# Cross-attention scores from stacked high and low float32r parts, through a scratch in HBM

## What is computed

```
q = axial_rope((layernorm(x) @ Wq), pos)       # per batch 128 x 32 x 8
k, v = split(ctx @ Wkv);  k = axial_rope(k, pos)
w = softmax(einsum('bqhd,bkhd->bhqk', q, k) / sqrt(8))
x = x + einsum('bhqk,bkhd->bqhd', w, v) @ Wout + bout
```

## Time and profile before

| | |
|---|---|
| median of 3 runs | 776.66 us |
| profiled execution | 777.8 us |
| its span, first to last instruction | 776.0 us |
| mean granted TensorE clock | 0.921 of 2.4 GHz |
| self-attention, last score product (L479) | starts 162 us |
| cross-attention, shifted products (L787) | 189.6 to 383.5 us |
| mixture of experts | from 397 us |

### The profile page before, as it was taken

The page is one execution under the profiler, slowest core; times in us unless marked ns, Lnnn a source line. Parts: engine busy times, 40 slices in busy tenths (PEclk is TensorE's granted clock), DMA queues, the critical chain, the costliest instruction groups (busy, mean ns, idle before and its releaser), DMA issues. The chain is left out here.

```text
span 776.0 us, 18811 instructions
## 1 busy us (share of the span) xinstructions
PE 687.4 (89%) x6959; PEld 528.3 (68%) x6959; DVE 401.1 (52%) x917; ACT 301.4 (39%) x676; POOL 359.9 (46%) x451
## 2 busy tenths in 40 slices
PE   4799999876999999999757979299999999999975
PEld 4677777444887887877633868267777777777864
DVE  3546554326366666665257599542222222221998
ACT  1455655321244445444517423023333333333422
POOL 2357653332122212210027435547777777775634
PEclk9889999887599999999858989779999999999989
DMA  7000000012112111111046930113333333333931
GB/s 200 13 13 9 11 13 9 13 18 35 19 20 37 27 34 29 30 34 18 3 157 188 238 87 1 41 55 103 103 102 103 103 107 102 106 102 114 349 102 34
DMA packets 49558, 55.88 MB, mean 72 GB/s; under 512 B 8462, under 2 KB 43776, under 8 KB 49472
## 3 DMA queue, kind: packets, MB, share of 16 engines
q1 hardware_dynamic: 39124, 33.16, 16.1%
q0 software_dynamic: 7584, 20.72, 8.3%
q10 hardware_dynamic: 2764, 0.80, 0.5%
HBM read 34.34 MB, written 14.55 MB: 63 GB/s over the span
## 5 line engine op out<-in xcount | busy, mean ns | idle before, releaser
L1563 PE MATMUL s<-wx,routed_out 128*128 x316 | 109.1, 468 | 1.0 <-ACT routed_out L1266 1.0
L1434 DVE TENSOR_TENSOR routed_out<-s,routed_out 128x176 f32<-128x176 f32 x79 | 27.0, 342 | 141.9 <-ACT routed_out L1271 141.9
L1198 POOL DMA_INDIRECT slot_rows<-stage,dest x79 | 78.0, 987 | 35.5 <-issue 19.5
L735 ACT ACTIVATE b_pt<-s 128x1024 f32<-128x1024 f32 x64 | 63.5, 1020 | 79.0 <-PE s L787 79.0
L1164 POOL DMA_INDIRECT routed_in<-normed_rows,token x79 | 77.7, 983 | 31.0 <-issue 20.3
L1582 PE MATMUL last<-wx,routed_out 88*128 x316 | 81.5, 380 | 0.7 <-DVE routed_out L1439 0.7
L717 DVE TENSOR_REDUCE b_mx<-s 128x8 f32<-128x1024 f32 x32 | 39.2, 1225 | 75.9 <-PE s L832 75.9
L1563 PEld LDWEIGHTS s<-wx,routed_out 128*128 128x128 f32 x316 | 54.9, 194 | 18.8 <-issue 2.4
L1172 POOL TENSOR_TENSOR h_full<-h_full,silu_gate 128x512 f32<-128x512 f32 (+1 forms) x24 | 31.8, 1326 | 57.0 <-ACT h_full L1242 57.0
L1447 DVE SCALAR_TENSOR_TENSOR x_sb<-wx,share,x_sb 128x256 f32<-128x256 f32 x64 | 51.7, 825 | 11.9 <-DMA wx<-slot_rows 10.1
L1582 PEld LDWEIGHTS last<-wx,routed_out 88*128 88x128 f32 x316 | 53.7, 190 | 5.7 <-issue 1.5
(11 more groups left out here) (265 smaller groups left out, 1568.9 us busy)
## 6 DMA issues: line engine op xcount, KB each, us to landing
wx<-slot_rows SPq DMA_DIRECT2D x16, 512.0 KB, 8.8
b_qk<-b_rot SPq DMA_DIRECT2D x128, 32.0 KB
wx<-in_w_gate SPq DMA_DIRECT2D x4, 528.0 KB
wx<-in_w_up SPq DMA_DIRECT2D x4, 528.0 KB
wx<-in_w_down SPq DMA_DIRECT2D x4, 528.0 KB
x_sb<-in_x SPq DMA_DIRECT2D x4, 512.0 KB, 6.2
normed_rows<-stage SPq DMA_DIRECT2D x4, 512.0 KB, 3.9
out<-x_sb SPq DMA_DIRECT2D x16, 128.0 KB, 1.8
```

Source lines behind the costliest of these rows:

```text
L735: nc.scalar.activation(pt[:, c % 2, u].rearrange("p h q -> p (h q)"), s2[:, u].rearrange("p a n -> p (a n)"), ACT.Exp, scale=HD_B ** -0.5) ...
L1198: nc.gpsimd.indirect_dma_start(out=slot_rows[:, :], out_offset=bass.IndirectOffsetOnAxis(ap=dest[:, n:n + 1].bitcast(U32), axis=0), in_=ys ...
L1563: last = nc.tensor.matmul(s2[:, n % 2, 0, 0:2 * FE], xT[:, n % 2, P * k:P * k + P], wx[:, bass.ds(e, 1), 2 * FE * k:2 * FE * k + 2 * FE].r ...
```

## The change

q and k, after the rotation, are each split into a high part (rounded to float32r, ACT) and a low part (the rest, POOL), in `parts`: q high, q low, k high, k low. A strip of `qk` then holds 24 rows: (q high, k high), (q low, k high), (q high, k low), 8 rows each, and rows 24 and 25 take the high and low part of the negated maxima beside ones in k. So one float32r matmul per score product gives high.high + low.high + high.low; the product low.low is left out. The stacking goes through a scratch of two slots in HBM, `stacks`: six DMAs a batch (128 partitions x two runs of 128 floats each) write it, and one DMA of 1 MB reads a whole slot into `qk`. The slots are filled once from `qk` (ones) at the first step. The low part of the maxima is a DVE subtraction. The preparation begins two steps earlier (FIRST = -10), the moments, normed x and projection of a batch two steps ahead of before, the rotation too, the split and the six DMAs in c = 2b - 6, the gather in 2b - 5.

```
@@ self_attention
...
-        return (t - 1 - BEHIND + 7) // 2 + 1
+        return (t - 1 - BEHIND + g["cross"]["ahead"]) // 2 + 1
...
@@ cross_attention
-    qk = sb("b_qk", [P, SL, 8, 2, P])
+    stacks = nc.dram_tensor("b_stacks", [2, P, 16 * P], F32, kind="Internal").ap()
+    qk = sb("b_qk", [P, SL, 8, 2, P], F32R)
     rot = sb("b_rot", [P, 2, 2, 2, P])
+    parts = sb("b_parts", [P, 2, 2, 4, P], F32R)
...
-    mT = sb("b_mT", [NH_B, 2, P])
+    mT = sb("b_mT", [NH_B, 2, 2, P], F32R)
...
-    FIRST, LAST = -8, NH + 2
-    STACK = 16 * 8
-
-    g["cross"] = {"init": init, "zeroed": zeroed, "mx": mx, "qk": qk, "v": v, "xcT_done": xcT_done, "steps": (FIRST, LAST)}
+    FIRST, LAST = -10, NH + 2
+    ROWS, SHIFT = 3 * HD_B, 3 * HD_B + 2
+    PIECES = 16 * 6
+
+    g["cross"] = {"init": init, "mx": mx, "qk": qk, "v": v, "xcT_done": xcT_done, "ahead": 9, "steps": (FIRST, LAST)}
...
+    def stacked(b, seg, part):
+
+        rows = stacks[b % 2].rearrange("(i r f) (x w t) -> r i (f x) w t", i=4, r=8, x=8, w=2)[2 * seg + part]
+        first, step = ((0, 2), (1, 1), (0, 3))[seg]
+        return rows, parts[:, b % 2, part, first:first + step + 1:step, :].bitcast(F32)
+
     def sync(sp, c):
-        b = batch(c + 8)
+        if c == FIRST:
+            for i in range(2):
+                sp.dma_start(stacks[i].rearrange("p (x w t) -> p x w t", x=8, w=2), qk[:, i].bitcast(F32)).then_inc(stack_out[i], 16)
+        b = batch(c + 10)
         if b is not None:
             need(sp, trx_done, b - 1)
             sp.dma_start(ctx[:, b % 2, :], io["ctx"][b]).then_inc(ctx_in[b % 2], 16)
         b = turned(c)
         if b is not None:
-            sp.wait_ge(mT_out, b + 1)
-            sp.dma_start(qk[HD_B:P:32, b % SL, :, 0, :], mT[:, b % 2, :]).then_inc(mrow_in[b % 2], 16)
+            for part, done in ((0, mT_out), (1, mT_lo)):
+                sp.wait_ge(done, b + 1)
+                sp.dma_start(qk[ROWS + part:P:32, b % SL, :, 0, :].bitcast(F32), mT[:, b % 2, part, :].bitcast(F32)).then_inc(mrow_in[b % 2], 16)
+        b = batch(c + 6)
+        if b is not None:
+            if b < 2:
+                sp.wait_ge(stack_out[b], 16)
+            else:
+                sp.wait_ge(qk_in[(b - 2) % SL], 16 * ((b - 2) // SL + 1))
+            sp.wait_ge(rot_lo, b + 1)
+            for seg in range(3):
+                for part in range(2):
+                    rows, src = stacked(b, seg, part)
+                    sp.dma_start(rows, src).then_inc(stack_out[b % 2], 16)
         b = batch(c + 5)
         if b is not None:
             need(sp, s2_done, 2 * (b - SL) + 2)
-            for part in range(2):
-                sp.wait_ge(rot_done, 2 * b + part + 1)
-                for i in range(4):
-                    sp.dma_start(qk[32 * i + 4 * part:32 * i + 4 * part + 4, b % SL], rot[32 * i:32 * i + 32, b % 2, part]).then_inc(qk_in[b % SL], 16)
+            sp.wait_ge(stack_out[b % 2], 16 + PIECES * (b // 2 + 1))
+            sp.dma_start(qk[:, b % SL].bitcast(F32), stacks[b % 2].rearrange("p (x w t) -> p x w t", x=8, w=2)).then_inc(qk_in[b % SL], 16)
 
     def gpsimd(pool, c):
-        b = batch(c + 8)
+        b = batch(c + 10)
         if b is not None:
             pool.wait_ge(ln_aggr, b + 1)
             nc.gpsimd.tensor_tensor(rstd[:, b % 2, 0:1], mv[:, b % 2, 1:2], g["ln_eps"][:, 0:1], ALU.add).then_inc(eps_done, 1)
             pool.wait_ge(eps_done, b + 1)
             nc.gpsimd.tensor_tensor(rstd[:, b % 2, 1:2], rstd[:, b % 2, 0:1], g["ln_pow"][:, 0:1], ALU.pow).then_inc(rstd_done, 1)
-        b = batch(c + 5)
-        if b is not None:
-            pool.wait_ge(cos_done, b + 1)
+        b = batch(c + 7)
+        if b is not None:
             pool.wait_ge(sin_done, b + 1)
-            if b >= 2:
-                pool.wait_ge(qk_in[(b - 2) % SL], STACK * ((b - 2) // SL + 1))
+            need(pool, rot_lo, b - 1)
             nc.gpsimd.tensor_tensor(rot[:, b % 2, 0], by_cos[:, 0], by_sin[:, 1], ALU.subtract).then_inc(rot_done, 1)
             nc.gpsimd.tensor_tensor(rot[:, b % 2, 1], by_cos[:, 1], by_sin[:, 0], ALU.add).then_inc(rot_done, 1)
-        b = batch(c + 7)
+        b = batch(c + 6)
+        if b is not None:
+            pool.wait_ge(rot_hi, b + 1)
+            pool.wait_ge(rot_done, 2 * b + 2)
+            halves = parts[:, b % 2].rearrange("p a (w h) t -> p a w h t", h=2)
+            nc.gpsimd.tensor_tensor(halves[:, :, :, 1, :], rot[:, b % 2], halves[:, :, :, 0, :].bitcast(F32), ALU.subtract).then_inc(rot_lo, 1)
+        b = batch(c + 9)
         if b is not None:
             pool.wait_ge(xn_done, b + 1)
             nc.gpsimd.tensor_tensor(x[:, b, :], x[:, b, :], g["ob"][:, 1, :], ALU.add).then_inc(ob_added, 1)
...
-        b = batch(c + 5)
+        b = batch(c + 7)
         if b is not None:
             dve.wait_ge(proj_done, b + 1)
             need(dve, rot_done, 2 * b)
-            for table, dst, done in ((1, by_cos, cos_done), (0, by_sin, sin_done)):
-                nc.vector.tensor_tensor(dst[:].rearrange("p a w t -> p (a w) t"), mid[:].rearrange("p (a t) -> p a t", a=4),
-                                        g["rope"][:, table, b, :].unsqueeze(1).broadcast_to([P, 4, P]), ALU.mult).then_inc(done, 1)
-        b = batch(c + 7)
+            for table, dst in ((1, by_cos), (0, by_sin)):
+                last = nc.vector.tensor_tensor(dst[:].rearrange("p a w t -> p (a w) t"), mid[:].rearrange("p (a t) -> p a t", a=4),
+                                        g["rope"][:, table, b, :].unsqueeze(1).broadcast_to([P, 4, P]), ALU.mult)
+            last.then_inc(sin_done, 1)
+...
+        b = turned(c)
+        if b is not None:
+            dve.wait_ge(mT_out, b + 1)
+            if b >= 2:
+                dve.wait_ge(mrow_in[b % 2], 32 * (b // 2))
+            nc.vector.tensor_tensor(mT[:, b % 2, 1, :], s1[0:NH_B, 0, 0:P], mT[:, b % 2, 0, :].bitcast(F32), ALU.subtract).then_inc(mT_lo, 1)
...
@@ scalar
+        b = batch(c + 6)
+        if b is not None:
+            act.wait_ge(rot_done, 2 * b + 2)
+            if b >= 2:
+                act.wait_ge(stack_out[b % 2], 16 + PIECES * (b // 2))
+            nc.scalar.copy(parts[:, b % 2].rearrange("p a (w h) t -> p a w h t", h=2)[:, :, :, 0, :], rot[:, b % 2]).then_inc(rot_hi, 1)
         exps(c, 0)
         b = turned(c)
         if b is not None:
             act.wait_ge(mT_done, b + 1)
             if b >= 2:
-                act.wait_ge(mrow_in[b % 2], 16 * (b // 2))
-            nc.scalar.copy(mT[:, b % 2, :], s1[0:NH_B, 0, 0:P]).then_inc(mT_out, 1)
+                act.wait_ge(mrow_in[b % 2], 32 * (b // 2))
+            nc.scalar.copy(mT[:, b % 2, 0, :], s1[0:NH_B, 0, 0:P]).then_inc(mT_out, 1)
         exps(c, 1)
         b = batch(c - 2)
...
@@ tensor, shifted
-            pe.wait_ge(mrow_in[(h // 2) % 2], 16 * (h // 4 + 1))
+            pe.wait_ge(mrow_in[(h // 2) % 2], 32 * (h // 4 + 1))
             pe.wait_ge(max_done, 2 * min(h + 2, NH - 1) + 1)
             need(pe, exp_done, 2 * h)
             need(pe, v_out, min((h + 1) // 2, NB - 1) + 1)
-            need(pe, xcT_done, min((h + 6) // 2, NB - 1) + 1)
+            need(pe, xcT_done, min((h + 8) // 2, NB - 1) + 1)
             need(pe, oT_done, (h - 4) // 2 + 1)
             for n in range(4):
                 for i in range(4):
-                    rows = slice(32 * i, 32 * i + HD_B + 1)
+                    rows = slice(32 * i, 32 * i + SHIFT)
                     pair = qk[rows, (h // 2) % SL, 4 * (h % 2) + n]
                     last = nc.tensor.matmul(second_bank(i)[:, P * n:P * n + P], pair[:, 1, :], pair[:, 0, :], start=(n == 0), stop=(n == 3))
...
@@ tensor, scores
-                pe.wait_ge(qk_in[b % SL], STACK * (b // SL + 1))
+                pe.wait_ge(qk_in[b % SL], 16 * (b // SL + 1))
             if h == 0:
                 pe.wait_ge(before["exp_done"], 2 * NB)
                 pe.wait_ge(before["max_done"], 2 * NB)
                 pe.wait_ge(before["mT_out"], NB)
             need(pe, max_done, 2 * h)
-            need(pe, mT_out, h // 2)
+            need(pe, mT_lo, h // 2)
             if half(c):
                 pe.wait_ge(exp_done, 2 * c + 1)
             for n in range(4):
                 for i in range(4):
-                    pair = qk[32 * i:32 * i + HD_B, b % SL, 4 * u + n]
+                    pair = qk[32 * i:32 * i + ROWS, b % SL, 4 * u + n]
                     last = nc.tensor.matmul(first_bank(i)[:, P * n:P * n + P], pair[:, 0, :], pair[:, 1, :], start=(n == 0), stop=(n == 3))
             last.then_inc(s1_done, 1)
 
...
```

More of the change, by code:

```diff
@@ L619, in cross_attention @@
     ctx_in = [sem(f"ctx_in{i}") for i in range(2)]
-    (zeroed, init, ln_stats, ln_aggr, eps_done, rstd_done, xn_done, trx_done, xcT_done, proj_done, cos_done, sin_done, rot_done,
-     ob_added, vp_done, v_out, s1_done, max_done, mT_done, mT_out, s2_done, exp_done, pv_done, sums_out, tb_done, rc_done,
+    stack_out = [sem(f"b_stack_out{i}") for i in range(2)]
```

(22 more changed lines are left out.)

18 lines of the change are left out of this document (10 added, 8 removed).

## The result

The changed kernel takes 830.7 us (median of 4 runs, 826.07 to 839.84) against 776.76 us: ratio 1.0719, 95% interval 1.0662 to 1.0777. The forecast was 823, range 770 to 875. The profiled execution is the shortest of the four, 826.07 us; its span is 824.3 us, 48.3 us more than the span of before, while the medians are 53.9 us apart.

What follows compares the result with a forecast made beforehand. PE bounds the old kernel; four DMA engines would bound the changed cross stage. Fill +3.9, start +5, period +34.8, tail -3.6, clock +6 sum to +46: 777.8 + 46 - 1.1 = 823 us, range 770 to 875.

Steps and rivals of the forecast that it cites:

- The four engines: Writing pieces to the scratch: strip outermost keeps each on four DMA engines, 10.3 us for a batch's six pieces.
- The period: Cross-attention stage: DMA work served in order takes 15.5 us a batch against PE's 10.9; +34.8 us over 13 batches.
- I charge nothing: High-part copy on ACT and split on POOL, a step ahead of use: 0 us; without cover each costs its length.
- The clock: Cross stage: a wait of about 4.6 us each batch invites PE's drop to 1.2 GHz; 0 to 16 us, taken as 6.
- The start: Up to the first shifted product: +3.9 us for the fill, +5 for its rows standing behind the third batch's pieces.
- The preparation two steps earlier: About 2.2 us of PE work per batch moves from cross stage into PE-bound self-attention steps: nothing in sum.
- The groups: Score groups on PE: 1.11 us becomes 0.67 (bounds 0.45 and 1.11), saving 1.8 us a batch.
- The added wait for mT_lo: In every second half scores() waits on PE for the DVE subtraction: 0.35 to 0.6 us.
- The tail: Last three batches, without pieces, run at PE's pace: -3.6 us.
- rival 1: Pieces spread over 16 engines at 0.4 us each, so DMA hides behind PE: 759 us, chance 0.11.
- rival 2: Score groups stay at 1.11 us, pieces hidden, new waits remain, 12.4 us a batch: 786 us, chance 0.05.
- the forecast's own range: 800 us (pieces 9.3 us, no clock loss) to 875 (pieces at 53 GB/s, 14.8 us), chance 0.79.

Runs made afterwards that it cites:

- Experiments 1 and 2: 1: changed kernel, scratch reordered to 16 outermost, four gathers, no fill: 758.5 us, again 751.93. 2: the same without the reordering: 835.05 us.
- experiment 3: Changed kernel with three of the six pieces a batch: 762.11 us; with every piece written twice, 12 a batch: 965.9 us.
- experiment 7: Kernel before, with only the fill added (two 1 MB copies from qk to a scratch in HBM): 783.59 us, ratio 1.0103.
- experiment 9: Changed kernel with spread pieces and no fill, plus the high part of the maxima copied by DVE instead of ACT: 756.26 us, ratio 0.9735.
- experiment 8: Kernel before, with only the preparation of each batch moved two steps earlier: 790.68 us, ratio 1.0156.

## Why the prediction was right, and where its terms were off

**The four engines: right.** The forecast's one decisive step was that a destination with four strips outermost keeps a piece on four engines. Experiments 1 and 2 differ in that alone, with the same bytes in packets of the same number and length, and stand at 0.970 to 0.984 against 1.072. Six pieces were taken at 10.3 us; at the 83 GB/s of the burst they are 9.5 us (786 KB), by the slope of experiment 3 they are 8.0.

**The period: 14.94 for 15.5 us.** The sum put pieces, landing, gather, rows and context in series. The pieces were cheaper by 0.8 to 2.3 us, the gather a little (351 GB/s for 340). Where the pieces are issued right behind a gather and its context load, the loop from pieces to pieces needs 13.3 + 0.9 = 14.2 us (285.40 to 298.72 and on to 299.5); an estimate of DMA's own period. What the sum did not have is the late split on POOL, behind the layer norm's small operations, which holds every second batch's pieces back for some 2 us beyond the gather. "I charge nothing" for POOL was right for its length and wrong for its place in the queue.

**The clock: there, but in another form.** The forecast had 34.8 us for the period and 6 for the clock on top, 40.8; the stage grew by 27.55. Against the spread version (rows of experiment 1 above) it is 52.7 us longer, of which PE's idle time is 40.9 - 13.8 = 27.1 us and the same instructions, slower at a granted clock of 0.80 for 0.95, 25.5. The slow clock is not simply added to DMA's period. In the batches that begin with a wait for the rows, PE then runs at 1.2 GHz in whole or in part and its slow products stand where waiting would; in the longest of them PE is busy for all of its 17.23 us. But it is then late itself with the product that the next split waits for, so that a part of the 0.7 us a batch above the 14.2 comes through the clock. The two feed each other, and no run here parts them: in one batch of two PE waits for DMA, and in the other its slow products take as long or longer.

**The start: mis-sized, with the stage the largest error.** The forecast had +3.9 for the fill and +5 ahead of the first shifted product; it was +21.2. PE's waits for DMA there, in the changed kernel:

```profile
174.52 2.09 PE L480 MATMUL s<-a_q,a_k 17*128 17x512 f32 x8 [5.87 <-DMA a_q<-a_mT]
...
201.08 1.12 PE L873 MATMUL s<-b_qk 24*128 24x128 f32 x16 [4.42 <-DMA b_qk<-b_stacks]
...
210.79 1.12 PE L828 MATMUL s<-b_qk 26*128 26x128 f32 x16 [7.76 <-DMA b_qk<-b_mT]
```

The step that failed is "its rows stand behind the third batch's pieces; I charge half their time". I followed only that one meeting. Already in the self-attention its own row of maxima (L348) stands behind the first batch's pieces: 5.87 us at 174.52. Then scores(0) waits 4.42 for a gather that comes behind six pieces, and shifted(0) 7.76 for its rows. From t = 10 to the first shifted product the kernels take 71.3 (before), 74.9 (preparation earlier), 76.8 (fill alone), 77.0 (pieces spread, no fill), 93.5 (no fill) and 95.5 us (changed). So the pieces on four engines cost 16.5 us here, the earlier preparation 3.6, and the fill 2.0 beside the pieces, 5.5 alone. The fill's stall was foreseen, its way was not: in the changed kernel it went through the context load (experiment 7), and the maxima row of the self-attention was late behind the first pieces instead.

**The preparation two steps earlier: wrong, cause open.** The moved work itself was well taken: "about 2.2 us" ahead of the first shifted product measured 2.6, with 1.0 of idle time, and 1.5 came back in the stage. But "nothing in sum" met +12 us (5 to 19) in the time; in the profile most of that is slow clock in the last halves, for which no cause was found.

**The groups: 0.60 us, for 0.67** taken between 0.45 and 1.11. The step behind it held: within a float32r group the first 8, 12 and 16 instructions end 0.44, 0.56 and 0.67 us behind the start, so a wave is 0.11 to 0.12 us, as in float32. The small rest of the gain lies in the first waves. PE alone needs 10.9 us a batch in the stage with its waits and its cold stretches, 10.62 steady, where 10.9 was predicted. The added wait for mT_lo measured 0.35 us, as the lower bound had it, and experiment 9 could not remove it.

**The tail: -0.5 for -3.6.** At the end PE has no DMA to wait for, but ran at a mean of 0.70 of its clock (28.49 us where before had 26.15). With the pieces spread the same five halves took 22.9 us at 2.4 GHz, 3.2 less than before: the term was right for a clock that the changed kernel did not have there.

So +21.2 + 27.55 + 2.3 - 2.8 = 48.3 stands against the +46 of the forecast: the total was nearer than its parts, since the start was 12 us too small and the stage 13 too large. That they cancel is luck. The four engines and a period well above PE's 10.9 us were foreseen with their reasons, and that is not. Three sums on record are a little off and decide nothing: rival 1's terms give 758.4 and not 759, rival 2's 785.5 and not 786, and the low end of the forecast's own range comes to 804 and not 800. Rival 1 (pieces that spread) did not happen by itself, but its number, 759 with the fill, is near what the kernel gives when they are made to spread and the fill goes: 758.5 and 751.9.

## What to carry to other kernels

Read how many engines a DMA gets from its own trace (end packets, share inside its burst) before adding traffic of that shape: pieces of 128 KB over all 128 partitions moved at 83 GB/s with 4 outermost in the destination and at 179 with 16, and the repair was another order of the same bytes in HBM. A saving on the engine that bounds is worth its length only while it goes on bounding; count what the new traffic costs in every place where an unrelated small transfer stands behind it, the start of the pipeline above all. And where DMA makes TensorE wait, look at the granted clock of the batch behind: here it was as low as 0.50, and PE was then late for work that the next transfer needed.

## What was not expected of the hardware

A gather of 1 MB from HBM in 8 KB runs moved at 351 GB/s in its middle and the fill at 411, more than the 340 of the store that was taken as the ceiling. Sixteen instructions of float32r on 24 to 26 rows take 0.60 us to the next group where 32 float32 ones on 8 or 9 rows take 1.11: 0.038 and 0.035 us an instruction, so that here the gain is nearly the halved count. And TensorE stayed at 1.2 GHz from 350 to 390 us in one kernel (experiment 8) although it was busy 95 to 100% of each ten microseconds.
